# Gated cross attention and local attention block: second tile's values, queries and transposes moved, probabilities transposed in pairs of heads

## What is computed

```
h = shift_token(x)
q, k, v = split(h @ wqkv, 3)             # 8 heads of 64
q, k = rotary_xpos(l2norm(q) * qs, l2norm(k) * ksc)
sim = einsum('bhwid,bhwjd->bhwij', bq, bk)          # windows of 128 rows, each sees itself and the one before
sim = where(mask, -inf, sim)
attn = softmax(sim, axis=-1)
x = x + einsum('bhwij,bhwjd->bhwid', attn, bv) @ wo
h = layernorm(shift_token(x)) * lg + lb
a, g = split(h @ w1 + b1, 2)
x = x + (a * gelu(g)) @ w2 + b2
```

## Time and profile before

| | us |
|---|---|
| median of 3 runs | 821.9 (819.35 to 823.16) |
| the profiled execution | 824.24 |
| its span, first to last instruction | 822.4 |
| mean granted TensorE clock | 0.964 of full speed |

### The profile page before, as it was taken

The page is one execution under the profiler, slowest core; times in us unless marked ns, Lnnn a source line. Parts: engine busy times, 40 slices in busy tenths (PEclk is TensorE's granted clock), DMA queues, the critical chain, the costliest instruction groups (busy, mean ns, idle before and its releaser), DMA issues.

```text
span 822.4 us, 17078 instructions
## 1 busy us (share of the span) xinstructions
PE 730.5 (89%) x4984; PEld 608.3 (74%) x4984; DVE 527.0 (64%) x1470; ACT 486.9 (59%) x1289; POOL 437.2 (53%) x592
## 2 busy tenths in 40 slices
PE   5898766989999999999998998999999999999967
PEld 4787654877878787878786877877777777777746
DVE  2898896384848484847475836657575766666732
ACT  2443425366767575757577665757575757575742
POOL 0433464473838383838383646738383737373712
PEclk9999987799999999999999998999999999999988
DMA  6444423160000000000101001010101010101000
GB/s 209 144 149 140 125 47 108 48 232 16 24 17 23 21 18 24 14 32 6 37 2 38 1 2 51 2 52 0 51 0 51 0 51 0 51 0 39 1 27 13
DMA packets 32786, 38.36 MB, mean 47 GB/s; under 512 B 8476, under 2 KB 22896, under 8 KB 32752
## 3 DMA queue, kind: packets, MB, share of 16 engines
q1 hardware_dynamic: 32752, 37.95, 14.4%
HBM read 29.55 MB, written 8.39 MB: 46 GB/s over the span
## 4 chain that ended last, share of the span: by engine, by line
PE 56%; DVE 13%; ACT 11%; issue 10%; POOL 5%; DMA 3%; SPq 1%; DVEq 1%; ACTq 0%; POOLq 0%
PE ps L422 39%; ACT pr L855 4%; PE ps L621 4%; PE ps L598 3%; DMA arena<-x 2%; PE ps L517 2%; DVE arena L955 2%; PE ps L580 2%; PE ps L592 1%; PE ps L415 1%; POOL xrs L1275 1%; ACT pT L861 1%; PE ps L625 1%; DVE sm L1153 1%; POOL pr L1357 1%
## 5 line engine op out<-in xcount | busy, mean ns | idle before, releaser
L1357 POOL TENSOR_SCALAR pr<-pr,rl 128x128 f32<-128x128 f32 (+1 forms) x256 | 107.6, 433 | 80.5 <-DVE rl L1159 80.4
L855 ACT ACTIVATE pr<-sm,mn 128x128 f32<-128x128 f32 (+1 forms) x256 | 113.4, 445 | 20.6 <-DVE mn L1153 20.1
L1153 DVE CUSTOM_DVE_ANT_0 sm<-ps,wmask 128x128 f32<-128x128 f32 (+1 forms) x256 | 79.9, 354 | 44.4 <-PE ps L598 38.5
L422 PE MATMUL ps<-hT_hi,w_hi 128*128 128x256 f32 (+1 forms) x352 | 103.4, 294 | 1.7 <-DVE hT_lo L1125 1.4
L422 PE MATMUL ps<-hT_hi,w_lo 128*128 128x256 f32 (+1 forms) x352 | 101.0, 287 | 0.0
L422 PE MATMUL ps<-hT_lo,w_hi 128*128 128x256 f32 (+1 forms) x352 | 100.2, 285 | 0.0
L1328 POOL TENSOR_TENSOR rn<-ss,nhalf 128x16 f32<-128x16 f32 x32 | 96.7, 3023 | 2.7
L813 ACT ACTIVATE sqb<-ps 128x512 f32<-128x512 f32 x64 | 38.0, 596 | 95.5 <-PE ps L422 88.6
L422 PE MATMUL ps<-wqkv_hi,yT_hi 128*128 128x512 f32 x192 | 80.3, 418 | 12.5 <-DVE arena L997 5.2
L1273 POOL TENSOR_SCALAR hrs<-hmv 128x2 f32<-128x2 f32 x16 | 3.1, 193 | 150.6 <-DVE hmv L1176 150.6
L1339 POOL TENSOR_TENSOR u_lo<-u_pair,u_hi 128x256 fp32r<-128x256 f32 x64 | 68.9, 1085 | 23.8 <-ACT u_hi L834 21.7
(11 more groups left out here) (148 smaller groups left out, 2129.8 us busy)
## 6 DMA issues: line engine op xcount, KB each, us to landing
arena<-x SPq DMA_DIRECT2D x16, 256.0 KB, 3.5
ystream<-arena SPq DMA_DIRECT2D x16, 256.0 KB, 2.0
y_next<-ystream SPq DMA_DIRECT2D x16, 256.0 KB, 2.8
y_res<-ystream SPq DMA_DIRECT2D x16, 256.0 KB, 2.6
arena<-L_ffn_w SPq DMA_DIRECT2D x6, 640.0 KB
arena<-ctx SPq DMA_DIRECT2D x8, 256.0 KB, 3.9
arena<-mask_BxSxS_ik SPq DMA_DIRECT2D x8, 256.0 KB, 2.8
xmid<-arena SPq DMA_DIRECT2D x8, 256.0 KB, 2.0
```

The costliest lines, as they stand in the source:

```text
L422: last = mm(out, lhsT(a), rhs(b), start=(start and i == 0), stop=(stop and i == 2))
L855: A(pr[:, h % NS, a:b], sm[:, h % NS, a:b], ACT.Exp, bias=mn[:, h, t:t + 1], scale=-1.0, accum_out=ls[:, h, t:t + 1]).then_inc(e_done, 1)
L1153: V.tensor_tensor_reduce(sm[:, h % NS, a:b], bank(h % SB)[:, a:b], wmask[:, a:b], 1.0, -NEG, ALU.add, ALU.min, mn[:, h, t:t + 1]).then_inc ...
L1357: G.tensor_scalar(pr[:, h % NS, a:b], pr[:, h % NS, a:b], rl[:, h, t:t + 1], 1.0, ALU.mult, ALU.mult).then_inc(pn_done, 1)
```

## The change

Four things are edited.

- Values of tile 1 go to bank 6 instead of bank 2. Their product no longer waits for `v_done` of tile 0; it waits for `o_done` of the step before (the bank's former reader), and `up(1)`, which also writes bank 6, waits for `v_done` of both tiles.
- Queries of tile 1 are copied out of bank 3 by DVE, between `gated(4)` and `gated(5)`, with a semaphore `q1_done` of their own.
- On PE `tr_heads(1, 0)` and `tr_heads(1, 1)` stand ahead of `up(5)` instead of behind it. On ACT `keys_T(1)` moves ahead of `high_u(3)` and `gelu(5)`, and a one-element EXP, which brings the table load with it, stands ahead of `high_u(4)`.
- The attention stretch on PE is written per pair of heads: `tr_probs` of both heads, then the scores of the pair two ahead, then one `down` part, then `weighted` of the pair before. Three more `down` parts run ahead of the first transposes.

The core of the diff:

```diff
                             else:
-                                pe.wait_ge(v_done, T * s + t)
+                                wait(pe, o_done, PAIRS * s)
...
-                        o = bank(i + j) if j < 2 else bank(2)
+                        o = bank(i + j) if j < 2 else bank(2 + 4 * t)
...
                     if c < 2:
                         pe.wait_ge(o_done, PAIRS * s)
+                        if c == 1 and la is not None:
+                            pe.wait_ge(v_done, T * (s + 1))
...
-                    for c in range(3, HC):
+                    for c in range(3, HC - 1):
                         up(c)
                 if A:
                     tr_heads(1, 0)
                     tr_heads(1, 1)
-                if A:
-                    pe.wait_ge(q_done, T * s + 1)
+                if F:
+                    up(HC - 1)
+                n = 0
+
+                def downs(upto):
+
+                    nonlocal n
+                    while F and n < upto:
+                        down(n)
+                        n += 1
+
+                if A:
+                    pe.wait_ge(q_done, s + 1)
                     pe.wait_ge(k_done, T * s + 1)
                     pe.wait_ge(v_done, T * (s + 1))
                     scores_own(0)
-                    pe.wait_ge(q_done, T * (s + 1))
+                    pe.wait_ge(q1_done, s + 1)
                     pe.wait_ge(k_done, T * (s + 1))
                     scores_both(0)
-                n = 0
-                if A and F:
-                    for n in range(HC - 1):
-                        down(n)
-                    n = HC - 1
-                if A:
-                    for h in range(HEADS + 1):
-                        if h in (0, 1, 3):
-                            scores_own((h + 3) // 2)
-                            scores_both((h + 3) // 2)
-                        if h < HEADS:
-                            tr_probs(h)
-                        if isinstance(s, int) and s in (0, NB) and h == HEADS - 1:
+                    downs(5)
+                    scores_own(1)
+                    scores_both(1)
+                    downs(8)
+                    for pair in range(PAIRS):
+                        tr_probs(2 * pair)
+                        tr_probs(2 * pair + 1)
+                        if pair + 2 < PAIRS:
+                            scores_own(pair + 2)
+                            scores_both(pair + 2)
+                        if isinstance(s, int) and s in (0, NB) and pair == PAIRS - 1:
                             bias_products(la)
-                        if F:
-                            while (n - HC + 1) * HEADS < (T * HC - 2 - HC + 1) * h:
-                                down(n)
-                                n += 1
-                        if h and h % 2 == 0:
-                            weighted(h // 2 - 1)
+                        downs(9 + pair if pair + 2 < PAIRS else 10)
+                        if pair:
+                            weighted(pair - 1)
+                    weighted(PAIRS - 1)
...
-                    A(vs[:, t, :], bank(2), ACT.Copy).then_inc(v_done, 1)
+                    A(vs[:, t, :], bank(2 + 4 * t), ACT.Copy).then_inc(v_done, 1)
...
+                if la is not None:
+                    keys_T(1)
+                if lf is not None:
                     high_u(3)
                     gelu(5)
                 if la is not None:
-                    queries_T(1)
-                    keys_T(1)
+                    A(table_touch[:, 1:2], table_touch[:, 0:1], ACT.Exp)
                 if lf is not None:
                     high_u(4)
...
+                def queries_T():
+                    dve.wait_ge(qk_tr, 2 * (T * s + 1) + 1)
+                    wait(dve, s_mm2, HEADS * s)
+                    V.tensor_copy(qT[:, :, P:S], bank(3).rearrange("p (c n) -> p c n", c=PAIRS)).then_inc(q1_done, 1)
...
                     gated(4)
+                if A:
+                    queries_T()
+                if F:
                     gated(5)
                     high_last_u()
```

More of the change, by code:

```diff
@@ L176, in build @@
         zeros_set, nhalf_set, tanh_done, prep_done = sem("zeros_set"), sem("nhalf_set"), sem("tanh_done"), sem("prep_done")
-        touch_set = sem("touch_set")
+        touch_set, q1_done = sem("touch_set"), sem("q1_done")
         dve_passed, pool_passed = sem("dve_passed"), sem("pool_passed")
@@ L834, in high_u @@
                     A(u[0][0:r, c, :], u_full[c % 4][0:r, :], ACT.Copy).then_inc(u_high, 1)
-                def queries_T(t):
-                    i = 0 if t == 0 else 3
-                    act.wait_ge(qk_tr, 2 * (T * s + t) + 1)
+                def queries_T():
+                    act.wait_ge(qk_tr, 2 * T * s + 1)
                     wait(act, s_mm2, HEADS * s)
-                    A(qT[:, :, t * P:(t + 1) * P], bank(i).rearrange("p (c n) -> p c n", c=PAIRS),
-                      ACT.Copy).then_inc(q_done, 1)
+                    A(qT[:, :, 0:P], bank(0).rearrange("p (c n) -> p c n", c=PAIRS), ACT.Copy).then_inc(q_done, 1)
                 def keys_T(t):
@@ L902, in step @@
                 if la is not None:
-                    queries_T(0)
+                    queries_T()
                 if lf is not None:
```

## The result

The changed kernel takes 883.7 us (median of 4 runs, 882.8 to 887.5), the kernel before in the same comparison 821.7 us (819.4 to 823.2). The ratio is 1.077 (95%: 1.073 to 1.081). It is slower, inside the range and 16 us above the 868 predicted.

What follows compares the result with a forecast made beforehand. A loop through four engines bounds the attention stretch, not PE. Loss of 2.74 us in fourteen steps (38.4), 3.3 in step 8, 4.0 in step 0: 45.7 on 824.24 gives 870, said as 868; range 850 to 890.

Steps and rivals of the forecast that it cites:

- the prediction's own bounds: Whole run: at least 850 us (1.9 us lost a step), at most 876 (about 3.6 a step).
- the clock's case: Rival "The clock falls": short PE idles halve the clock in ten steps of fifteen, 17 us more, 885; chance 0.12.
- The loop over four engines: Attention stretch: scores, DVE minimum and reciprocal, POOL scaling, PE transposes take 2.96 us; two turns of 3.34 in a row.
- sign asked for: Steady step after: period near 43.6 us, `low_u(4)` wait about 1, odd heads' transposes about 3.3 apart, DVE and ACT idle.
- its refutation: Transposes of heads 1, 3 and 5 standing 2.8 us apart or less: loop not the bound, prediction wrong.
- its 0.21: Front of a step: tile 1's values in bank 6 let `up(0)` start 0.21 us earlier, carried to the end.
- Steps 8 and 0: Step 8 loses 3.3 us; step 0 loses 4.0: 1.5 for query copy and first scores, 2.5 for the pairs' loop.
- late `low_u(4)`: Front: the table load starts `high_u(4)` 1.16 us later; `low_u(4)` ends at 611.05, PE idle from about 610.1 to 611.10.
- Table load: ACT, ahead of `high_u(4)`: 1.40 us from load to next instruction; the skill's drain of about 1.38 left out.
- 0.8 busy in the same place: Trace of before, where the changed step idles PE (616 to 627): 0.8 busy at full clock, held against the falling clock.
- Faster: Rival: ACT bounds the attention stretch, the loop costs nothing, about 1.0 us a step gained, 807 us; chance 0.08.
- Half the price: Rival: only the tail or only the loop is real, 1.2 to 1.5 us a step, 840 to 846 us; chance 0.06.

Runs made afterwards that it cites:

- x1_pairs_alone: The kernel before with only PE's new order from the fifth `down` part on (attention in pairs); 879.6 us.
- x8_both_between: The changed kernel with both the scores and the weighted products put between the two heads' transposes; 822.8 us.
- x7_sums_first: The changed kernel with DVE's reciprocals of heads 3 and 5 put ahead of the row minima of heads 4 and 6; 872.8 us.
- x11_no_touch: The changed kernel without the one-element EXP (the table touch) alone, keys staying ahead of `high_u(3)`; 880.7 us.
- x12_keys_later: The changed kernel with only the keys' copy moved behind `high_u(3)` on ACT, the table touch kept; 881.5 us.

## Why the prediction was right, and where its sizes were off

**Sign and mechanism.** Right, and shown by edits, at too small a size. By the prediction's own bounds the loop could give 876 us at most; 883.7 lies above them. It is inside the range only because that was stretched to 890 for the clock's case, which did not come in the steady steps. That much of the hit is luck.

The loop over four engines is the cost (`x1_pairs_alone` carries 3.1 of 3.4), both places named by the prediction, the scores behind two heads' transposes and the weighted product behind the scores, are needed for it (`x8_both_between`), and DVE's queue is a link (`x7_sums_first`). Nearly every sign asked for is in the rows above: half copy behind a table load, `down` part waiting 1.03 us, transposes of head 3 waiting 1.16, minima idle 1.57, ACT idle 1.72 and 1.59. Heads 1 and 3 are 3.44 apart and heads 3 and 5 3.73, where about 3.3 was said for both. Of these distances the first tells nothing, as it was 3.70 before; what the prediction named as its refutation, 2.8 or less, could only have been read from both.

**Sum of a step.** 2.74 us was forecast and 3.40 found. On the prediction's clock: `up(0)` at 597.84 (597.85 was said), half copy of the last chunk at 609.82 (609.59), second pair's scores at 611.73 (611.34), third pair's at 615.16 (614.68), fourth pair's at 618.59 (618.02), `exps(6)` at 621.59 (621.02), `weighted(3)` at 627.42 (626.77); the figures in brackets are those of the prediction less its 0.21. So the error has two sources, and every link between them is right within 0.02 us.

- The *front*, 0.39. The first product after a wait takes 0.23 us to the next one and not 0.12 (639.16 to 639.39), which takes back half of the 0.21; the fifth `down` part and its scores lose 0.10 in the same way (0.55 apart, not 0.45); the rest is 0.12 between keys and table load, since `high_u(3)` takes 0.43 to the next instruction (648.82 to 649.25) and not 0.31, and 0.06 between the half copy and the `down` part.
- *Transposes ahead of scores or of a weighted product*, 0.09 to 0.11 each time, three times in the step. The prediction took 0.38 from two heads' transposes back to back, but in the new order other products follow the odd head. The trace of before had the right row, in PE's timeline:

```profile
612.78 0.33 PE L607 MATMUL ps<-ident,pr 128*128 128x128 f32 x1 [0.48 <-POOL pr L1357]
613.26 0.38 PE L592 MATMUL ps<-kT,qT 64*128 64x128 f32 x2
...
614.64 0.36 PE L422 MATMUL ps<-w_hi,u_hi 128*128 128x256 f32 x1
```

From these transposes to the scores it is 0.48, and so it is at 656.00 and 656.48 after. The wait ahead of them is not the cause. The 0.1 us lies behind the third transpose of the group: from there it is 0.21 to the scores (613.05 to 613.26) and 0.11 to further transposes (618.31 to 618.42). Head 1's transposes of before wait too (614.34) and are 0.30 from the `down` part behind them (614.64). And in `x8_both_between`, where a group starts at 654.92 right behind a product and with no wait, its third transpose has the same 0.21 to the scores:

```profile
655.14 0.27 PE L611 MATMUL ps<-ident,pr 128*128 128x128 f32 x1
655.35 0.49 PE L594 MATMUL ps<-kT,qT 64*128 64x128 f32 x4
```

So the price goes with what stands behind the group: in these rows 0.48 ahead of scores, 0.38 ahead of further transposes, 0.30 ahead of a `down` part. The prediction kept 0.1 us for each wait of PE in its upper bound. In the front that was the term that it lacked; in the loop the amount was right and the reason was not. In the fourteen steps the error is 48.1 - 38.4 = 9.7 us.

**Steps 8 and 0.** The terms that failed most for their size. Step 8 cost 4.5 us instead of 3.3 and step 0 6.1 instead of 4.0. From its middle to the first shift product, step 0 reads so in the windows of the changed kernel:

```profile
116.00:168.00 52.00, 33.27 (x185) 25.23 (x185) 24.14 (x76) 18.91 (x54) 21.92 (x29) 0.67 0.23 68
```

and in those of the kernel before:

```profile
116.00:161.70 45.70, 31.98 (x185) 24.54 (x184) 23.95 (x75) 19.33 (x54) 22.29 (x29) 0.74 0.26 78
```

The work is the same but for 1.3 us on PE, which is busy for longer at a mean granted clock of 0.67 instead of 0.74; the other 5.0 of the 6.3 us between the two windows is PE idle. PE's timelines tell where they lie, from the bias products (L517) to the last weighted product, after the change:

```profile
149.72 7.15 PE L517 MATMUL ps<-lgb,arena 128*128 128x1 f32 x44
...
156.79 1.12 PE L623 MATMUL ps<-pT,vs 128*64 128x256 f32 x4
...
159.23 1.12 PE L623 MATMUL ps<-pT,vs 128*64 128x256 f32 x4 [0.89 <-ACT pT L868]
```

and before:

```profile
146.33 7.45 PE L517 MATMUL ps<-lgb,arena 128*128 128x1 f32 x44 [0.74 <-DMA arena<-L_ffn_w]
...
153.71 1.12 PE L621 MATMUL ps<-pT,vs 128*64 128x256 f32 x4
```

The second pair's scores start 1.54 us later than before (134.07 and 132.53), as the 1.5 said. From there to the bias products the loop costs 1.85, less than the 2.5 said. But between the bias products and the last weighted product another 2.13 come, since two weighted products now stand behind them, 2.44 apart. The prediction had this term for step 8 and none for step 0, which has the bias products too. The last 0.62 come between there and the first shift product. In step 8 the two weighted products are 2.44 apart as well (528.11 and 530.55). The granted clock had a part that was not measured by itself: in step 0 it stood at half from 121.3 to 141.8 us, where before it stood at half for 6.8 us twice, with 3.4 us at full clock between. The two steps bring 3.3 us more than forecast.

**From the sum to 868.** 9.7 and 3.3, less 0.3 behind the last step, added to the forecast 45.7, make up the 58.5 us between the two profiles. The prediction then took off 2.3 us, since its profiled execution lay above the median of before; that of the changed kernel lies 0.9 below its own. Together 16 us, the whole distance between 868 and 883.7.

**Cause of the late `low_u(4)`.** The time came out nearly right (611.18 us where 611.10 was said, 610.89 less the 0.21) but the cause only half. "1.16 us later" was put on the table load; the queue of POOL, with the keys' new place in front of it, ends nearly as late by itself (`x11_no_touch`, `x12_keys_later`). For the forecast this made no difference, for a repair it does: taking out the touch gives 3 us in 884, taking out both 15.

**Table load.** The prediction left the drain of the Trainium skill (ScalarE: Activation LUTs, section "What ACT_TABLE_LOAD costs") out of its sum. The trace agrees with that choice: the load starts at 649.74 and the half copy at 651.14, 1.40 us for both the load and the touch.

**Rivals.** "The clock falls" was given 885, nearly the measured time, and is still not what happened in the steady steps: the windows of the changed kernel from 200 to 470 and from 586 to 851 us, which hold all ten of them, show the full clock.

```profile
200.00:470.00 270.00, 234.81 (x1706) 191.61 (x1706) 160.40 (x468) 164.24 (x456) 145.84 (x196) 1.00 0.05 18
...
586.00:851.00 265.00, 230.73 (x1673) 188.61 (x1671) 162.60 (x462) 160.62 (x443) 143.23 (x192) 1.00 0.07 23
```

Where it acted, in single steps of the experiments, it cost 1.3 to 1.6 us and not 1.7. The "0.8 busy in the same place" was too low: in the kernel before PE is busy for 10.19 of the 11.00 us from 616 to 627, so that trace says less against this rival than the prediction took from it. "Faster" fails at the point that it named: ACT is idle for 0.69 us before `exps(4)` at 658.31, since the minimum of head 4 is not there (0.8 was said). The 616.7 given there for the end of the minimum is the time at which `exps(4)` can start; by the earlier trace rows the minimum ends at 614.89 + 1.43 = 616.32. "Half the price" fails because both halves are real: 1.4 to 1.5 us each.

## What to carry to other kernels

In a loop over in-order queues, ask of each instruction that is moved behind a wait what the other engines have queued behind its result: here the same transposes, minima and copies cost 3.4 us a step or nothing, by two places in one queue. Take the price of a link from a row with the neighbours that it will have: the same wait ahead, the same kind of instruction behind. And before one removes a delay, look for the second that ends at the same time; here either repair alone gave 0.42 or 0.19 us, both 1.27.

## What the runs showed of the hardware that was not expected

- A transpose took 0.21 us to scores behind it, 0.11 to a further transpose and 0.03 to a `down` part (613.05, 618.31 and 614.61 in the kernel before); the first and the last are the same with and without a wait ahead of the group.
- A first product after a wait took 0.23 us to the next of its kind (639.16), where 0.12 is the pitch within a row of them; behind scores it took 0.22 without a wait (649.78).
- In `x1_pairs_alone` a stretch with PE busy for 1.73 us of 3.40 was followed by half clock for 3.4 us, in two steady steps of ten; the changed kernel, with the same order of the pairs, shows none. One such fall cost 1.56 us of a 44 us step.
- The EXP table's load cost 1.40 us up to the half copy behind it, the touch included, but only 0.42 us of a step came back when the touch was taken out and the load moved to the first `exps` (`x11_no_touch`), since another delay ended nearly as late.
